# ScalarE copies the O bank of a finished block one exponential later in its program

## The reference, cut to what matters

```python
q = (x @ Wq.T).reshape(d, n, h)      # d = 128, n = 3327, h = 8
k = (x @ Wk.T).reshape(d, n, h)
v = (x @ Wv.T).reshape(d, n, h)
a = jnp.einsum('dnh,dmh->dnm', q, k) * scale
a = a + spatial_encoding + edge_encoding     # both are adj
a = jax.nn.softmax(a, axis=2)
out = jnp.einsum('dnm,dmh->dnh', a, v)
out = out.reshape(n, h * d)
return out @ Wo.T
```

## Time and profile before

| what | value |
|---|---|
| device time, three runs | 13901.7, 13902.25, 13903.08 us (median 13902.25) |
| span of the profiled execution | 13904.2 us (its device time is not listed apart from this span) |
| PE busy | 13474.1 us, 97% |
| DVE busy | 13175.3 us, 95% |
| ACT busy | 13116.0 us, 94% |
| POOL busy | 1509.8 us, 11% |
| granted TensorE clock | 0.992 of full speed over the span |

### The profile page before, as it was taken

How to read it: one execution, slowest core, us unless ns; L and a number is a source line. 1 busy time by engine, 2 the same in 40 slices (tenths; PEclk the granted TensorE clock), 3 DMA queues, 4 the chain that set the end, 5 groups by cost and what they waited for, 6 DMA issues and landing times. The chain is left out here.

```text
span 13904.2 us, 337069 instructions
## 1 busy us (share of the span) xinstructions
PE 13474.1 (97%) x130699; PEld 4162.7 (30%) x130699; DVE 13175.3 (95%) x27486; ACT 13116.0 (94%) x26756; POOL 1509.8 (11%) x1220
## 2 busy tenths in 40 slices
PE   5989999999999999999999999999999999999998
PEld 3522222222222222222222222222222222222224
DVE  6689999999999999999999999999999999999992
ACT  2379999999999999999999999999999999999997
POOL 2220101111110111111111111111111111111110
PEclk8999999999999999999999999999999999999999
DMA  8975656656565655656566565656656565665653
GB/s 285 254 158 140 148 139 145 142 138 149 139 149 138 146 142 138 149 137 149 138 145 143 138 149 137 149 139 143 144 138 150 138 149 137 145 143 139 148 138 92
DMA packets 1951493, 2060.35 MB, mean 148 GB/s; under 512 B 756537, under 2 KB 1704800, under 8 KB 1943488
## 3 DMA queue, kind: packets, MB, share of 16 engines
q1 hardware_dynamic: 1949062, 2035.58, 62.4%
q10 hardware_dynamic: 824, 3.21, 0.1%
HBM read 1929.05 MB, written 109.05 MB: 147 GB/s over the span
## 5 line engine op out<-in xcount | busy, mean ns | idle before, releaser
L239 DVE CUSTOM_DVE_ANT_0 swept<-X,adj_row 128x832 f32<-128x832 f32 x13312 | 12838.9, 1021 | 349.5 <-PE X L261 282.4
L1000 ACT ACTIVATE prob<-S 128x476 f32<-128x476 f32 x23296 | 11598.4, 569 | 155.0 <-PE S L1068 43.7
L1090 PE MATMUL O<-prob,v_pad 128*32 128x238 f32 (+1 forms) x77648 | 6677.1, 416 | 21.8 <-ACT o_sb L1026 19.1
L1068 PE MATMUL S<-q_blk,k_res 60*128 60x476 f16 x23296 | 5963.2, 368 | 35.9 <-DVE q_blk L1037 15.2
L261 PE MATMUL X<-mk,mq 40*128 40x416 f16 x26624 | 5757.7, 344 | 153.1 <-DVE m_part L239 80.5
L1068 PEld LDWEIGHTS S<-q_blk,k_res 60*128 60x128 f16 x23296 | 1666.6, 93 | 3512.7 <-ACT prob L1000 1476.9
L261 PEld LDWEIGHTS X<-mk,mq 40*128 40x128 f16 x26624 | 1541.8, 93 | 3244.4 <-DVE m_part L239 2729.2
L1090 PEld LDWEIGHTS O<-prob,v_pad 128*32 128x32 f32 x77648 | 1528.5, 108 | 2661.9 <-issue 2403.2
L991 ACT ACTIVATE S<-adj_key 128x476 f32<-128x476 f32 (+1 forms) x2912 | 1701.2, 584 | 35.0 <-issue 4.3
L211 POOL TENSOR_SCALAR m_neg<-m_full 128x16 f32<-128x16 f32 x208 | 52.5, 253 | 11327.4 <-DVE m_full L222 11327.2
L961 POOL TENSOR_SCALAR q_blk<-q_blk 24x1904 f16<-24x1904 f16 (+1 forms) x222 | 1108.4, 4993 | 142.9 <-DMA q_blk<-q_planes 126.0
(11 more groups left out here) (85 smaller groups left out, 1059.1 us busy)
## 6 DMA issues: line engine op xcount, KB each, us to landing
adj_row<-in_adj SPq DMA_DIRECT2D x1600, 416.0 KB, 3.8
adj_key<-adj_by_key SPq DMA_DIRECT2D x2496, 238.0 KB, 3.9
mk<-k_planes SPq DMA_DIRECT2D x1664, 104.0 KB
adj_key<-adj_by_key SPq DMA_DIRECT2D x416, 236.0 KB, 3.9
mk<-k_planes SPq DMA_DIRECT2D x1664, 52.0 KB
row<-in_adj SPq DMA_DIRECT2D x47, 1663.5 KB, 8.2
adj_by_key<-aT SPq DMA_DIRECT2D x26, 1664.0 KB, 12.0
mq<-q_planes SPq DMA_DIRECT2D x416, 64.0 KB
```

The lines of the kernel that those rows point to most:

```text
L239: nc.vector.tensor_tensor_reduce(out=swept[u % 2][:], in0=x_, in1=adj_row[gi % 4][:].rearrange("p (a b) -> p a b", a=2), scale=1.0, scalar ...
L1000: nc.scalar.activation(prob[born(j, d // 4) % QR][:, d % 4, 0:w], S[b][:, 0:w], ACT.Exp, scale=2.0).then_inc(s_e[b], 1)
L1068: nc.tensor.matmul(S[b][:, 0:w], k_res[base:base + KR, d // 2, s * P:(s + 1) * P], q_blk[n % 2][base:base + KR, d // 2, 0:w], start=False, ...
L1090: done = nc.tensor.matmul(O[32 * d:32 * d + 32, cols], v_pad[:, s, 4 * q + d, :], prob[born(j, q) % QR][:, d, cols], start=first, stop=Tru ...
```

## The change

The copy of O stands one exponential later in ScalarE's program. Nothing else differs: TensorE's and SyncE's lists of instructions are the same row for row.

```diff
@@ -1016,7 +1016,7 @@
                                 if d == GH - 1 and LATER[j % 3] == late and j + 3 < JOBS:
                                     bias(j + 3)
 
-                        copied = {place(104 * (n + 1) - 1): n for n in range(NG * NBL)}
+                        copied = {place(104 * (n + 1) - 1) + 1: n for n in range(NG * NBL)}
                         for f in range(2 * CYCLE * CYCLES + 1):
                             if f in copied:
                                 n = copied[f]
```

## The result

| | before | changed |
|---|---|---|
| device time, median of 6 runs | 13901.98 us | 13948.74 us |
| lowest and highest | 13898.72, 13905.62 | 13946.32, 13950.94 |
| span of the profiled execution | 13904.2 us | 13949.2 us |

The changed kernel is 46.8 us slower: ratio 1.0033, 95% interval 1.0022 to 1.0045. The profiled executions differ by 45.0 us. The forecast was 13950.

A forecast was written before the change was run, and what follows sets the result against it. Three nearly full engines holding each other by short waits were taken as the bound; 12.8 + 15.2 + 9.5 + 6.5 + 2.0 + 1.6 = 47.6 us on 13902.25 gave 13950, range 13922 to 13968.

The forecast's parts named there:

- the ninth end: Block end at the ninth copy, two scores ahead: product, score, exponential and sweep all shift by 0.51 us; 25 such, 12.8 us.
- the walk: One block end of each kind followed forward, product moved by the copy's delay, other instructions shifted as needed; sum 47.6 us.
- ends like the second: The 25 block ends like that at the second copy, two scores ahead: everything shifts by 0.61 us, 15.2 us in all.
- two-score ends: 50 block ends where TensorE has done two scores ahead of the waiting product: delay lost whole, 12.8 and 15.2 us.
- three-score ends: 61 block ends with three or more scores ahead of the waiting product: delay partly made good; 9.5, 6.5, 2.0, 1.6 us.
- those like the first: 25 block ends like that at the first copy, three scores ahead and a double product: 0.38 us each, 9.5 us.
- the fifth end: Block end at the fifth copy: ScalarE 0.35 us late at first, 0.2 three exponentials on; 0.17 taken, 12 such, 2.0 us.
- The wait for o_sb about 122 us: TensorE's weight loads would wait for the copies into o_sb about 59.8 + 62 = 122 us, or more than 100.
- The store and the transfers cost nothing: SP's store waits for the later copy, half a microsecond in front of loads issued jobs ahead: costed at nothing.
- The rival that the delay is made good later: Idle time on VectorE and ScalarE absorbs the delay: 13921, or 13902 if all; chance 0.14 for 13902 to 13930.
- The rival by occupancy: ScalarE, busy 98.7%, sets the time and its work is unchanged: no change; no chance of its own given.
- The rival of the faster kernel: At 61 ends the earlier exponential frees its bank 0.45 us sooner and the product's wait costs nothing: 13881; chance 0.04.

The follow-up runs named there:

- the run with these ends alone: Copy one exponential later only at the 50 block ends with two scores ahead of the waiting product, against the kernel before: 13928.71 us, 28.4 us more.
- the run with the wait alone: Kernel before, ScalarE's program unchanged; only each block's first product on TensorE waits for one exponential more, the one following the copy: 13940.33 us, 40.0 us more.

## Why the prediction was right

The mechanism was that of the forecast, and the total lies 1.3 us below it (13948.74 against 13950). That closeness is in part luck: the shifts of the exponentials add up to 44.5 us and the profiled executions differ by 45.0, where the sum had 47.6.

- *The copy is 0.51 late at the ninth end, 0.61 at the second.* The ninth copy was 0.54 late (from the bias to it 3.44 us, 2.90 before), a little more than forecast, and the product came 0.04 sooner behind its start, which the walk did not have; the two nearly cancel, and the cost is 0.50, and 0.57 to 0.64 at ends like the second. No run shows why the copy is shorter there. The lateness of the moved exponential's own score belonged in the sum: without it the walk would have had 22 us at the 50 ends, and 28.4 were measured.
- *At two-score ends all three engines shift together, so that nothing is made good.* Shown by the idle times of 0.54, 0.93 and 0.80 us, by the next cycle of 40.15, and by the run with these ends alone.
- *At three-score ends a part is made good.* Right, and mis-sized upward in each term: summed over the ends of a kind, 8.1 us instead of 9.5 for those like the first (half of them are 0.24 and not 0.38, where I had walked both halves to one number), 5.9 for 6.5, 1.6 for 2.0, 1.3 for 1.6. The sum of 19.6 measured 16.8. The walk had the course right: the exponentials that read the scores behind the first product are 0.44 late, the ones after them 0.28 (0.48 and 0.25 to 0.3 in the walk), and at the fifth end the lateness falls from 0.33 to 0.13.
- *The wait for o_sb about 122 us*: 120.3. *A block 116.6*: 116.60. *The cycle 41.2*: 41.23.
- *The store and the transfers cost nothing.* Not tested by themselves. In the run with the wait alone the store is as early as before, and the ends like the ninth cost 0.50 all the same, as in the whole change; so there no cost of the later store is seen.
- The rival that the delay is made good later falls with the per-end costs that stay the same over 180 exponentials. The rival by occupancy had ScalarE at 98.7% set the time and no change; the run with the wait alone slows the kernel by 40 us and leaves ScalarE's instructions alone. The rival of the faster kernel counted on a product that waits beside a sweep at the three-score ends and so costs nothing; no kind of end gained.

The trace sum of 44.5 and the medians' 46.8 differ by 2.3 us, within the spread of 4 to 7 us of the runs of one kernel.

## What to carry to other kernels

Where several engines are nearly always busy (here 97 to 99% between the first and the last copy) and hold one another in a fixed order, look for the place where one instruction releases another engine's queue, and follow in the timeline what stands behind it: in this kernel a delay of that release was lost whole where all three engines stood waiting behind it, and in part where more work lay ready ahead of the waiting instruction; a second delay was then lost whole. Of the three places tried for the copy the old one is the best: one exponential later it holds up the product, one earlier it waits for its own input and holds up ScalarE.

## What the runs showed of the hardware

Two ScalarE instructions overlap by about as much when the first is short as when it is long. With the copy of 8 columns at its old place, at the ninth block's end:

```profile
1832.55 0.21 ACT L1026 ACTIVATE o_sb<-O 128x8 f32<-128x8 f32 x1
1832.62 2.17 ACT L1000 ACTIVATE prob<-S 128x476 f32<-128x476 f32 x4
```

The copy lasts 0.21 us and the next exponential starts 0.07 behind its start, an overlap of 0.14; with the full copy it is 0.60 and 0.45, an overlap of 0.15. Over all ends, where the next score is ready, the run with the short copy moved has medians of 0.172 and 0.057, the changed kernel with the full copy 0.562 and 0.447: an overlap of 0.115 in both.
